# Routed experts in pieces of 128 rows instead of 256, fetched six pieces ahead, with the row lists made in bf16

## The reference

```python
scores = x @ Wg + bg                      # (4096 tokens, 8 experts)
for e in range(8):                        # the chosen tokens only matter
    h = gelu(x @ W1[e] + b1[e])           # 128 -> 512
    y = h @ W2[e] + b2[e]                 # 512 -> 128
    output = output + y * combine_w[..., e:e+1]   # layer 1: two experts, weighed
# layers 2 and 3: the output is y of the single best expert
```

## Time and profile before

| | |
|---|---|
| median of 3 runs | 5160.9 us (5158.99 to 5167.45) |
| the profiled execution | 5161.76 us, its span 5159.4 us |
| TensorE busy, share of the span | 4267.9 us, 83% |
| VectorE / ScalarE / GpSimd busy | 69% / 48% / 55% |
| granted TensorE clock, mean | 0.912 of 2.4 GHz |

### The profile page before, as it was taken

The page is one execution under the profiler, slowest core; times in us unless marked ns, Lnnn a source line. Parts: engine busy times, 40 slices in busy tenths (PEclk is TensorE's granted clock), DMA queues, the critical chain, the costliest instruction groups (busy, mean ns, idle before and its releaser), DMA issues. The chain is left out here.

```text
span 5159.4 us, 163839 instructions
## 1 busy us (share of the span) xinstructions
PE 4267.9 (83%) x70247; PEld 3443.9 (67%) x70439; DVE 3539.8 (69%) x5684; ACT 2485.6 (48%) x3536; POOL 2847.7 (55%) x2159
## 2 busy tenths in 40 slices
PE   6996899899998999899989999899977666565765
PEld 5884777677777777677767777777753566464565
DVE  4445888888888888888888888888855522633442
ACT  2222555556555555565555656555542233432532
POOL 2233676676767766767667676777730055144024
PEclk9786999999999999999999999999998677666967
DMA  0001222222222222232222222222210111122022
GB/s 23 0 0 57 66 59 66 59 76 70 60 64 76 63 66 60 66 80 60 59 66 76 69 60 66 63 65 65 61 40 9 55 39 39 40 78 47 0 72 64
DMA packets 215524, 284.07 MB, mean 55 GB/s; under 512 B 59550, under 2 KB 104388, under 8 KB 214084
## 3 DMA queue, kind: packets, MB, share of 16 engines
q1 hardware_dynamic: 203972, 251.85, 18.8%
q0 software_dynamic: 10880, 22.30, 1.8%
HBM read 56.26 MB, written 19.66 MB: 15 GB/s over the span
## 5 line engine op out<-in xcount | busy, mean ns | idle before, releaser
L1512 POOL TENSOR_TENSOR local_rot<-local_rot,local_sines 128x512 f32<-128x512 f32 x768 | 955.3, 1279 | 952.9 <-DVE local_sines L1591 952.9
L1520 POOL TENSOR_TENSOR local_inv_norm<-local_norm2c,minus_half 128x16 f32<-128x16 f32 x384 | 1127.8, 2937 | 32.0
L1400 ACT COPY local_v_tile<-local_bank 128x1024 f32<-128x1024 f32 x192 | 195.5, 1018 | 809.0 <-PE local_bank L1179 809.0
L1177 PE MATMUL local_bank<-local_wqkv_hi,local_ys_hi 128*128 128x512 f32 x1152 | 474.2, 412 | 40.3 <-DVE local_gates L1640 18.3
L1252 PE MATMUL local_bank<-ident,local_normed 128*128 128x128 f32 x3072 | 406.2, 275 | 102.5 <-ACT local_probs_t L1410 91.8
L1591 DVE TENSOR_TENSOR local_rot<-local_bank,local_table 128x1024 f32<-128x1024 f32 x384 | 466.8, 1216 | 21.1 <-ACT local_squares L1405 13.8
L1591 DVE TENSOR_TENSOR local_sines<-local_bank,local_table 128x1024 f32<-128x1024 f32 x384 | 465.5, 1212 | 0.0
L1596 DVE TENSOR_REDUCE local_norm<-local_squares 128x16 f32<-128x1024 f32 x384 | 463.5, 1207 | 0.0
L1581 DVE TENSOR_TENSOR local_normed<-local_rot,local_inv_norm 128x1024 f32<-128x1024 f32 x384 | 452.0, 1217 | 12.1 <-POOL local_inv_norm L1520 7.2
L1179 PE MATMUL local_bank<-local_wqkv_hi,local_ys_lo 128*128 128x512 f32 x1152 | 454.9, 395 | 0.2 <-issue 0.2
L1178 PE MATMUL local_bank<-local_wqkv_lo,local_ys_hi 128*128 128x512 f32 x1152 | 453.8, 394 | 0.0
(11 more groups left out here) (416 smaller groups left out, 9027.8 us busy)
## 6 DMA issues: line engine op xcount, KB each, us to landing
local_vals<-local_v_tile SPq DMA_DIRECT2D x1152, 130.0 KB, 2.4
local_vals<-local_v_tile SPq DMA_DIRECT2D x672, 65.0 KB, 2.1
local_stage<-in_L_ffn_Wqkv SPq DMA_DIRECT2D x6, 1536.0 KB, 7.8
moe_at_row<-y_rows SPq DMA_DIRECT2D x32, 256.0 KB, 4.8
moe_w<-in_L_ffn_W SPq DMA_DIRECT2D x3, 2048.0 KB, 9.8
x_rows<-moe_rows SPq DMA_DIRECT2D x12, 512.0 KB, 3.2
local_wo<-in_L_ffn_Wo SPq DMA_DIRECT2D x6, 512.0 KB, 8.4
moe_taken<-x_rows,moe_take POOLq DMA_INDIRECT x170, 2.6
```

The source lines that it names most:

```text
L1177: nc.tensor.matmul(out, hi, wqkv_hi[:, d0:d1], start=True, stop=False)
L1512: last = nc.gpsimd.tensor_tensor(of_heads(rot, a)[:, :, to], of_heads(rot, a)[:, :, to], of_heads(sines, a)[:, :, of], ALU.add)
L1520: nc.gpsimd.tensor_tensor(inv_norm[:, cols], norm2c[:, cols], g.minus_half[:, cols], ALU.pow).then_inc(q["inv_norms_ready"], 1)
```

## The change

Pieces have 128 rows: 71 of them in moe1, 39 in moe2 and in moe3. Each piece is fetched by one indirect DMA and sent by one. GpSimd fetches six pieces before the first send, and keeps that distance; `taken` and `made` have eight buffers, `hid`'s source banks four. Each piece splits its expert's weights anew, as before, so that this happens once per 128 rows. The matmuls of `up` keep the weights stationary and move 128 columns; `down` is 4 matmuls.

The lists are made in bf16: a row's number is 128 times its tile plus its place in the tile plus one, and these two parts are multiplied into `at_col` by GpSimd (two new instructions a chunk), VectorE makes `at_col` ahead of `at_row` and no longer multiplies, and one bf16 matmul a tile moves both parts side by side. VectorE adds the parts.

VectorE gives out the shift of a group while it takes the statistics of the second group after it. ScalarE writes the rows of three groups, VectorE those of the fourth, ahead of its third copy to `XH`. The results are read back into the space of the weights instead of that of `at_row`; `row_id` has a column more, for the place in the tile.

```diff
-    SLOTS = 2 * P
-    NJ = (NT * P + E * (SLOTS - 1)) // SLOTS
-    COLS = NJ * SLOTS // P
-    GROUPS, CHUNKS, BUFS = 4, 4, 4
+    NJ = (NT * P + E * (P - 1)) // P
+    GROUPS, CHUNKS, AHEAD, BUFS = 4, 4, 6, 8
...
-        at_row = ph.sb("at_row", [P, NT, P])
-        at_col = ph.sb("at_col", [P, NT, COLS])
-        listed = ph.sb("listed", [P, COLS])
-        take = ph.sb("take", [P, COLS], I32)
-        put = ph.sb("put", [P, COLS], I32)
+        at_row = ph.sb("at_row", [P, NT, P], BF16)
+        at_col = ph.sb("at_col", [P, NT, NJ], BF16)
+        row_of = ph.sb("row_of", [P, NT, 2, NJ], BF16)
+        part_listed = ph.sb("part_listed", [P, NJ])
+        whole_listed = ph.sb("whole_listed", [P, NJ])
...
-        taken = ph.sb("taken", [P, BUFS, 2, P])
-        made = ph.sb("made", [P, BUFS, 2, P])
-        xt_hi, xt_lo = (ph.sb(n, [P, 2, SLOTS], F32R) for n in ("xt_hi", "xt_lo"))
-        hid = ph.sb("hid", [P, 2, FC, SLOTS])
-        back = at_row
+        taken = ph.sb("taken", [P, BUFS, P])
+        made = ph.sb("made", [P, BUFS, P])
+        xt_hi, xt_lo = (ph.sb(n, [P, 2, P], F32R) for n in ("xt_hi", "xt_lo"))
+        hid = ph.sb("hid", [P, 2, FC, P])
+        back = [v[:].rearrange("p e b f -> p (e b) f") for v in (w1, w2)]
...
-                for i in range(GROUPS):
+                for i in range(GROUPS - 1):
...
-                    for h in range(2):
-                        act.wait_ge(q["hid_done"], 2 * j + h + 1)
-                        for b in (2 * h, 2 * h + 1):
-                            last = nc.scalar.activation(hid[:, j % 2, b, :], bank[:, 2 + 2 * (j % 2) + h, (b % 2) * SLOTS:(b % 2 + 1) * SLOTS], gelu,
-                                                        bias=b1[:, bass.ds(e * FC + b, 1)])
-                        last.then_inc(q["gelu_done"], 1)
+                    act.wait_ge(q["hid_done"], j + 1)
+                    for b in range(FC):
+                        last = nc.scalar.activation(hid[:, j % 2, b, :], bank[:, 2 + j % 4, b * P:(b + 1) * P], gelu, bias=b1[:, bass.ds(e * FC + b, 1)])
+                    last.then_inc(q["gelu_done"], 1)
...
+                        pe.wait_ge(q["row_of_ready"], t // (NT // CHUNKS) + 1)
+                    last = nc.tensor.matmul(bank[:, LISTS, 0:2 * NJ], at_row[:, t, :], row_of[:, t, :, :].rearrange("p a c -> p (a c)"), start=(t == 0), stop=(t == NT - 1))
...
-                    for h in range(2):
-                        last = nc.tensor.transpose(bank[:, j % 2, h * P:(h + 1) * P], taken[:, j % BUFS, h, :], g.ident[:])
-                    last.then_inc(q["x_turned"], 1)
+                    nc.tensor.transpose(bank[:, j % 2, 0:P], taken[:, j % BUFS, :], g.ident[:]).then_inc(q["x_turned"], 1)
...
                 def up(j):
                     pe.wait_ge(q["lo_ready"], j + 1)
                     pe.wait_ge(q["wt_lo_ready"], j + 1)
-                    for h in range(2):
-                        if j >= 2:
-                            pe.wait_ge(q["gelu_done"], 2 * (j - 2) + h + 1)
-                        for b in (2 * h, 2 * h + 1):
-                            out = bank[:, 2 + 2 * (j % 2) + h, (b % 2) * SLOTS:(b % 2 + 1) * SLOTS]
-                            nc.tensor.matmul(out, wt_hi[:, j % 2, b, :], xt_hi[:, j % 2, :], start=True, stop=False)
-                            nc.tensor.matmul(out, wt_lo[:, j % 2, b, :], xt_hi[:, j % 2, :], start=False, stop=False)
-                            last = nc.tensor.matmul(out, wt_hi[:, j % 2, b, :], xt_lo[:, j % 2, :], start=False, stop=True)
-                        last.then_inc(q["hid_done"], 1)
+                    if j >= 4:
+                        pe.wait_ge(q["gelu_done"], j - 3)
+                    for b in range(FC):
+                        out = bank[:, 2 + j % 4, b * P:(b + 1) * P]
+                        nc.tensor.matmul(out, wt_hi[:, j % 2, b, :], xt_hi[:, j % 2, :], start=True, stop=False)
+                        nc.tensor.matmul(out, wt_lo[:, j % 2, b, :], xt_hi[:, j % 2, :], start=False, stop=False)
+                        last = nc.tensor.matmul(out, wt_hi[:, j % 2, b, :], xt_lo[:, j % 2, :], start=False, stop=True)
+                    last.then_inc(q["hid_done"], 1)
 
                 def down(j):
                     e = pe.value_load(owner[0:1, j:j + 1], min_val=0, max_val=E - 1)
-                    pe.wait_ge(q["gelu_done"], 2 * j + 2)
+                    pe.wait_ge(q["gelu_done"], j + 1)
                     if j >= 2:
                         pe.wait_ge(q["y_ready"], j - 1)
-                    for h in range(2):
-                        for b in range(FC):
-                            last = nc.tensor.matmul(bank[:, 6 + j % 2, h * P:(h + 1) * P], hid[:, j % 2, b, h * P:(h + 1) * P],
-                                                    w2[:, bass.ds(e, 1), b, :], start=(b == 0), stop=(b == FC - 1))
+                    for b in range(FC):
+                        last = nc.tensor.matmul(bank[:, 6 + j % 2, 0:P], hid[:, j % 2, b, :], w2[:, bass.ds(e, 1), b, :], start=(b == 0), stop=(b == FC - 1))
                     last.then_inc(q["y_done"], 1)
...
+                pool.wait_ge(q["small_loaded"], SMALL_LOADS)
+                SPAN = NT // CHUNKS
+                for c in range(CHUNKS):
+                    part = slice(c * SPAN, (c + 1) * SPAN)
+                    pool.wait_ge(q["cols_ready"], c + 1)
+                    nc.gpsimd.tensor_tensor(row_of[:, part, 0, :], at_col[:, part, :], row_id[:, 1 + c * SPAN:1 + (c + 1) * SPAN].unsqueeze(2).to_broadcast([P, SPAN, NJ]), ALU.mult)
+                    nc.gpsimd.tensor_scalar(row_of[:, part, 1, :], at_col[:, part, :], row_id[:, 0:1], None, ALU.mult).then_inc(q["row_of_ready"], 1)
                 pool.wait_ge(q["rows_stored"], 16 * GROUPS)
                 pool.wait_ge(q["take_ready"], 1)
 
                 def fetch(j):
                     if j >= BUFS:
                         pool.wait_ge(q["x_turned"], j - BUFS + 1)
-                    for h in range(2):
-                        c = 2 * j + h
-                        nc.gpsimd.indirect_dma_start(taken[:, j % BUFS, h, :], None, g.x_rows,
-                                                     bass.IndirectOffsetOnAxis(ap=take[:, c:c + 1], axis=0)).then_inc(fetched[j % BUFS], 16)
+                    nc.gpsimd.indirect_dma_start(taken[:, j % BUFS, :], None, g.x_rows,
+                                                 bass.IndirectOffsetOnAxis(ap=take[:, j:j + 1], axis=0)).then_inc(fetched[j % BUFS], 16)
 
                 def send(j):
                     pool.wait_ge(q["y_ready"], j + 1)
-                    for h in range(2):
-                        c = 2 * j + h
-                        nc.gpsimd.indirect_dma_start(g.y_rows, bass.IndirectOffsetOnAxis(ap=put[:, c:c + 1], axis=0),
-                                                     made[:, j % BUFS, h, :], None).then_inc(sent[j % BUFS], 16)
-
-                for j in range(BUFS - 1):
+                    nc.gpsimd.indirect_dma_start(g.y_rows, bass.IndirectOffsetOnAxis(ap=put[:, j:j + 1], axis=0),
+                                                 made[:, j % BUFS, :], None).then_inc(sent[j % BUFS], 16)
+
+                for j in range(AHEAD):
                     fetch(j)
                 pool.wait_ge(q["put_ready"], 1)
                 for j in range(NJ):
-                    if j + BUFS - 1 < NJ:
-                        fetch(j + BUFS - 1)
+                    if j + AHEAD < NJ:
+                        fetch(j + AHEAD)
                     send(j)
...
+                def shifts(i):
+                    part = slice(i * PER_GROUP, (i + 1) * PER_GROUP)
+                    dve.wait_ge(q["rstd_ready"], i + 1)
+                    nc.vector.scalar_tensor_tensor(shift[:, part], mean_var[:, part, 0], -1.0, rstd[:, part], ALU.mult, ALU.mult).then_inc(q["shift_ready"], 1)
...
+                    if i >= 2:
+                        shifts(i - 2)
...
+                    if s == 2:
+                        dve.wait_ge(q["rows_ready"], GROUPS - 1)
+                        for t in range(TOKEN_TILES - PER_GROUP, TOKEN_TILES):
+                            last = nc.vector.tensor_scalar(rows[:, t, :], token(t), mean_var[:, t, 0:1], rstd[:, t:t + 1], ALU.subtract, ALU.mult)
+                        last.then_inc(q["rows_ready"], 1)
...
+                    nc.vector.tensor_tensor(at_col[:, part, :], count[:, 0:NJ].unsqueeze(1).to_broadcast([P, SPAN, NJ]),
+                                            pos[:, 1, part].unsqueeze(2).to_broadcast([P, SPAN, NJ]), ALU.is_equal).then_inc(q["cols_ready"], 1)
                     nc.vector.tensor_tensor(at_row[:, part, :], count[:].unsqueeze(1).to_broadcast([P, SPAN, P]),
-                                            pos[:, 2, part].unsqueeze(2).to_broadcast([P, SPAN, P]), ALU.is_equal)
-                    done(nc.vector.tensor_tensor(at_col[:, part, :], count[:, 0:COLS].unsqueeze(1).to_broadcast([P, SPAN, COLS]),
```

(10 more changed lines are left out.)

48 lines of the change are left out of this document (23 added, 25 removed).

## The result

The changed kernel takes 4973.0 us (median of four runs, 4965.0 to 4974.6) against 5161.4 beside it: a ratio of 0.963, 95% interval 0.9614 to 0.9647, so 188 us less. The forecast was 4945. Its profiled execution took 4972.8 us over a span of 4971.0, at a mean granted clock of 0.93.

The account below looks back on a forecast made before the run. Fetch-to-finish latency, not an engine, was taken to bound the expert stages, with GpSimd's DMAs next. Gains of 179.0 (stages), 28.9 (lists) and 8.4 us (rows), 216 in all, off 5161.8 give 4945 us; own range 4915 to 4985, wider 4912 to 5045.

Parts of the forecast that it names:

- The ring and the bound after it: Expert stages: the send-to-finish latency cycle stops binding, 1.4 us a piece; GpSimd's two DMAs bind at 2.70 us.
- TensorE at 2.5 us a piece, nothing gained from half the columns: Expert stages: 21 matmul records at 0.12 us a piece; `up` gains nothing from moving 128 columns instead of 256.
- The clock: Expert stages: TensorE, without long gaps, gets the high clock, granted near 1 against 0.77 in moe1 before.
- The stages: Expert stages of moe1, moe2, moe3: 196.4, 110.0 and 110.0 us, together a gain of 179.0 us.
- The rows: Row-writing phases: ScalarE and TensorE start 4.7 us earlier, net 2.8 three times, together a gain of 8.4 us.
- The lists: Making the row lists in bf16: gains of 12.9 us in moe1, 8.0 each in moe2 and moe3, together 28.9.
- upper end: Lists of moe1: GpSimd's two products at 2.62 ns an element, 6.0 us a chunk; gain down to 4 us.
- lower end: Lists of moe1: GpSimd's two products at 0.93 ns an element, 2.1 us a chunk; gain up to 20 us.
- the rival's 12 us a chunk: Lists: GpSimd slower still on bf16; moe1 loses 19, moe2 and moe3 some 3 each, total 4999 us; chance 0.04.
- Small stalls: Expert stages: engine chains in lockstep with two buffers, mean 3.1 us a piece, 60 us back, 5005; chance 0.18.
- float32r loses its rate: `up` at 128 columns: TensorE binds at 4.05 us a piece, 5146 us, or 5094 with partial overlap; chance 0.15.

Follow-up runs that it names:

- e2: The changed kernel with three pieces fetched ahead instead of six, buffers still eight: 5240.6 us, ratio 1.016.
- e3: The changed kernel sending back only even-numbered pieces, results read from the stored rows, so the output differs: 4958.4 us, ratio 0.961.
- e4: The changed kernel with every fetch made twice, the second into a tile nobody reads, three indirect DMAs a piece: 5147.4 us in a single execution.
- e9: The changed kernel with nothing edited, run again on another chip: 5092.4 us, ratio 0.987.
- e1: The kernel before, still 256 rows a piece, with six fetches ahead instead of three and eight buffers: 5015.8 us, ratio 0.973.
- e11: Same file as e5 (the changed kernel, both list products moved off GpSimd), run on the chip of e9: 5073.5 us, ratio 0.983.
- e5: The changed kernel with GpSimd's two list products moved, the position one to VectorE, the row one to ScalarE: 5072.3 us, ratio 0.982.
- e8: The changed kernel with four pieces fetched ahead instead of six: 5088.6 us, ratio 0.986.
- e7: The changed kernel with the float32 lists of the kernel before: 5089.8 us, ratio 0.987.
- e10: Same file as e8 (the changed kernel, four pieces fetched ahead), run on the chip of e9: 5088.0 us, ratio 0.986.

## Why the prediction was right, and where it was not

- *The ring and the bound after it*: right. The ring went (TensorE's waits for rows from 77.3 us to 8.4), e2 brought it back with 5240.6 us, and GpSimd became the slowest engine, at 1.33 us a DMA for the 1.35 taken. e3 and e4 move the stage with the number of its DMAs.
- *TensorE at 2.5 us a piece, nothing gained from half the columns*: right. The pitch of `up` is 0.114 us for the 0.118 carried over from 256 columns; e3 shows how near this second bound is. The rule cited there of the Trainium skill (TensorE: Matmul & The Clock Gate, section LDWEIGHTS), by which a weight load takes its columns over 1.2 GHz, 0.107 us for 128, agrees with this at the high clock. At the low one e9's matmuls, each with its load, come 0.21 us apart, so the clock counts as well.
- *The clock*: right for the chips without late increments, 0.96 in moe1's stage, 0.91 and 0.92 in the other two. Much of the stage's gain is this: e1 does the matmuls of before in 144 us instead of 183.
- *The stages*: 418.1 us for 416.4 forecast, 177 gained for 179. *The rows*: from the first load of the phase to the first step of the lists 49.2 us in moe1 against 51.8, 2.6 gained for 2.8; moe2 gained 2.6 as well and moe3 1.2, 6.4 for the 8.4 forecast.
- *The lists*: the term that was mis-sized. Forecast 28.9 us, measured 2.7: moe1 lost 3.7, the others gained 3.2 each. That is 26 of the 28 us between 4945 and 4973. The step that failed is the price of GpSimd's two products, 3.9 us a chunk, and with it the overlap: VectorE's 14.0 us for the four chunks were taken to run beside them for nothing. The products took 10.4, 9.3, 7.6 and 5.2 us. By themselves, as in the last chunk, they are 5.2: the product of two tensors is 2.08 us for the 2.6 forecast, but the one with a scalar, priced at half of the other, is 3.16 for 1.3. The rest, up to 5.1 us a chunk, is VectorE's time, as worked out above: GpSimd is busy without a gap, as the forecast said of moe1, and what it adds up to is nearly the sum of both engines, 4 x 5.24 + 4 x (1.34 + 2.28) = 35.4 us, for 33.8 from the first `at_col` to the last product. In moe2 and moe3 the forecast had VectorE as the bound and 9.3 us; they take 14.1. The forecast's upper end, 6.0 us a chunk, was therefore no bound. Its lower end was none either: with VectorE's 14.0 us as the bound the gain could be 16 us at most, not 20. In the same way the rival's 12 us a chunk, which is 3.3 in moe2 and moe3, would leave their lists at 16.4 us, a gain of 1 and not a loss of 3. The rule of the Trainium skill (GPSIMD Engine Reference, section 3.1) that was weighed there, 2.5 us for the product of two tensors, lies above the 2.08 that the trace shows with VectorE nearly idle and far below the 4.00 beside it.

In e11 no list work is on GpSimd, and the timeline shows the same instructions by themselves:

```profile
4098.40 1.33 DVE L520 TENSOR_TENSOR moe_at_col<-moe_count,moe_pos 128x1136 bf16<-128x1136 f32 x1
...
4099.77 1.24 ACT L267 ACTIVATE moe_row_of<-moe_at_col,moe_row_id 128x1136 bf16<-128x1136 bf16 x1 [3.40 <-DVE moe_at_col L520]
4101.85 1.34 DVE L525 TENSOR_TENSOR moe_row_of<-moe_at_col,moe_row_id 128x1136 bf16<-128x1136 bf16 x1
...
4114.07 0.20 DVE L529 TENSOR_SCALAR moe_owner_f<-moe_owner_f 128x71 f32<-128x71 f32 x1
```

1.33 us instead of up to 4.02 for `at_col`, 0.20 instead of 2.27 for the step over 71 elements, and 1.24 us on ScalarE for what took GpSimd 3.2 to 6.4. With this the lists take 44.6 us in the three phases, against 68.9 before: 24.3 gained, near the 28.9 of the forecast. On one chip e11 is 19 us faster than e9, and e5 16 faster than e8. The bf16 lists as the change builds them are worth about nothing: e7, with the old ones, takes 5089.8 beside the 5088.6 of e8, whose shorter look-ahead e10 found to cost nothing there.

- *The rivals.* "Small stalls" was priced at 5005 and "float32r loses its rate" at 5094 to 5146. e9's 5092 lies between them and has neither cause: pitch 0.11 at the high clock, fetches in time. No rival held a chip on which TensorE's increments come late. The forecast was right for the chip that measured it, and that it was this kind of chip is luck: on C the same file leaves the range (4912 to 5045) and gains 1.3% instead of 3.7%.

*What stays open*: why the increments come late on B, C and D. Shown is that the edits don't make them, that they hit the expert stages with 128 rows and no earlier phase, and that a pause each piece doesn't end them. That the chip makes them is the nearest reading, but each chip was used in one session, so a cause that came with the session is not excluded. Nor can the traces tell increments held back from matmuls that really ended late, as TensorE's ends are modelled. Whether 256-row pieces with the look-ahead (e1, 5015.8 on A) escape it was not tried on such a chip. The kernel before keeps its time on all four, which speaks for it, since late increments would lengthen its ring; there is no trace of it from B, C or D. If so e1 would be the faster kernel there, and that is argued, not measured.

The version to keep is e5/e11, the changed kernel with the lists' products on VectorE and ScalarE: 5073.5 us on C, faster than both the kernel before (5160.6) and the changed one (5092.4) there. That is 0.4% under the changed kernel, with no overlap of the times (5068.4 to 5075.0 against 5087.2 to 5096.3). It did not run on a chip without late increments; by its lists, 21.6 us shorter than the changed kernel's, I estimate 4950 to 4955 us there.

## What to carry to other kernels

When a stage is bound by a ring of latencies, first fetch further ahead: here that one number gave 145 of 188 us, and smaller pieces without it made the kernel slower than before. Elementwise work put on GpSimd beside a busy VectorE is not free time: here the stage took nearly the sum of both, so price it as that sum, and look whether ScalarE is idle. When a run surprises, run the unedited kernel beside it on the same chip before explaining it by the edit; the kernel before is no control for this, since it was equally fast on all four chips. And before counting late events in a trace, check by their consumers that they are not lost records.

## What the runs showed of the hardware that was not expected

- The same file takes 4973 us on one chip and 5092 on another, with the same instructions and nearly equal granted clocks over the whole (0.930 and 0.921).
- In the traces of three chips 57 to 123 of 447 semaphore increments of TensorE groups appear 1 to 4.0 us after the modelled end of their matmuls, in bursts of up to four within 0.3 us, while TensorE goes on, and 51 to 93 times in a run a consumer stands idle for over 1 us. On two others, under the same feeding, none does.
- In the same three chips' expert stages 45 to 104 of some 447 increment records of each of TensorE, ScalarE and VectorE are missing from the trace, though their consumers go on.
- GpSimd and VectorE hold each other up at bf16 elementwise work, by lengths that fit taking turns: 1.33 to 4.02 us for one and the same VectorE instruction, 3.16 to 6.37 us for a GpSimd product of 1136 elements with a scalar, 2.08 to 4.00 for one of two tensors. ScalarE beside VectorE keeps its 1.24 us for the product with a scalar.
- An indirect DMA of 128 rows costs GpSimd 0.94 to 1.0 us in most cases and up to 1.5 in some, 1.02 on average over the changed kernel, and 0.30 of issue, whether it gathers (median 0.97) or scatters (0.99).
